# Graph attention on one core: the values of group 1 in other banks, the first group transposed in three steps, a warm-up before the first weights

## What is computed

```python
h = jnp.maximum(_layernorm(x, axis=-1), 0.0)
output = jnp.einsum('bni,io->bno', feature, weight)
q = jnp.einsum('bni,io->bno', feature, wq)
k = jnp.einsum('bni,io->bno', feature, wk)
alpha = jnp.einsum('bno,bmo->bnm', q, k)
alpha = jnp.maximum(alpha, 0.0) * (graph != 0).astype(alpha.dtype)
alpha = jax.nn.softmax(alpha, axis=1)
return jnp.einsum('bnm,bmo->bno', alpha, output)   # feature is h; x is added
```

## Time and profile before

| | before |
|---|---|
| median of 3 runs | 421.62 us (420.26 to 421.87) |
| profiled execution | 420.8 us, of which the span of the trace is 419.0 us |
| PE busy | 406.6 us (97%) |
| DVE busy | 282.9 us (68%) |
| ACT busy | 253.3 us (60%) |
| POOL busy | 298.2 us (71%) |
| chain that ended last | PE 81%, POOL 9%, DMA 3%, DVE 3% |
| DMA in the first slice (10.5 us) | 286 GB/s |

### The profile page before, as it was taken

How to read it: one execution, slowest core, us unless ns; L and a number is a source line. 1 busy time by engine, 2 the same in 40 slices (tenths; PEclk the granted TensorE clock), 3 DMA queues, 4 the chain that set the end, 5 groups by cost and what they waited for, 6 DMA issues and landing times.

```text
span 419.0 us, 9187 instructions
## 1 busy us (share of the span) xinstructions
PE 406.6 (97%) x3499; PEld 314.8 (75%) x3499; DVE 282.9 (68%) x504; ACT 253.3 (60%) x517; POOL 298.2 (71%) x315
## 2 busy tenths in 40 slices
PE   5999997999999999999999999999999999999996
PEld 4434543779889797979889797979889797978452
DVE  4786566475866768685876768676777677456353
ACT  4478774657485666667485666667586765523421
POOL 0379887979979797979879797979889796130320
PEclk9999999999999999999999999999999999999999
DMA  7965748996969797896978598996988599261022
GB/s 286 364 91 97 194 81 212 202 219 177 191 216 178 221 165 206 199 210 178 196 238 157 154 213 219 194 207 180 187 251 151 157 228 221 51 107 59 0 103 100
DMA packets 157368, 73.97 MB, mean 177 GB/s; under 512 B 131216, under 2 KB 139408, under 8 KB 157328
## 3 DMA queue, kind: packets, MB, share of 16 engines
q1 hardware_dynamic: 156752, 72.37, 75.5%
q10 hardware_dynamic: 576, 1.05, 0.7%
HBM read 24.12 MB, written 16.78 MB: 98 GB/s over the span
## 4 chain that ended last, share of the span: by engine, by line
PE 81%; POOL 9%; DMA 3%; DVE 3%; ACT 1%; SPq 1%; issue 1%; DVEq 0%; POOLq 0%; ACTq 0%
PE bank L1041 9%; PE bank L1027 9%; PE bank L1026 9%; PE bank L1042 9%; PE bank L1024 9%; PE bank L1039 9%; PE s_bank L1055 3%; PE s_bank L1053 3%; PE s_bank L1054 3%; POOL hn_lo L375 2%; PE bank L1060 2%; PE bank L1062 2%; PE bank L1061 2%; DMA x_sb<-in_x 2%; POOL hn_lo L401 2%; PE bank L1160 2%
## 5 line engine op out<-in xcount | busy, mean ns | idle before, releaser
L375 POOL TENSOR_TENSOR hn_lo<-h,hn_hi 128x512 f16<-128x512 f32 x64 | 73.4, 1159 | 41.0 <-ACT hn_hi L512 40.7
L502 ACT ACTIVATE h<-x_sb,shift,rstd 128x512 f32<-128x512 f32 x64 | 49.8, 803 | 51.4 <-POOL shift L370 51.4
L401 POOL TENSOR_TENSOR hn_lo<-s,hn_hi 128x512 f16<-128x512 f32 x52 | 58.6, 1159 | 0.0
L1024 PE MATMUL bank<-hT_hi,mt_hi 128*128 128x256 f16 x208 | 56.7, 273 | 0.0
L1027 PE MATMUL bank<-hT_hi,mt_lo 128*128 128x256 f16 x208 | 56.7, 273 | 0.0
L1041 PE MATMUL bank<-wt_lo,hT_hi 128*128 128x256 f16 x208 | 56.7, 273 | 0.0
L1042 PE MATMUL bank<-wt_hi,hT_lo 128*128 128x256 f16 x208 | 56.7, 273 | 0.0
L1026 PE MATMUL bank<-hT_lo,mt_hi 128*128 128x256 f16 x208 | 56.7, 273 | 0.0
L1039 PE MATMUL bank<-wt_hi,hT_hi 128*128 128x256 f16 x208 | 56.7, 273 | 0.0
L517 ACT ACTIVATE hn_hi<-s 128x512 f16<-128x512 f32 x52 | 32.5, 628 | 36.4 <-POOL s L390 23.9
L407 POOL TENSOR_TENSOR probs<-exps,row_inv 128x512 f32<-128x512 f32 x16 | 16.8, 1049 | 47.3 <-DVE row_inv L829 47.3
(11 more groups left out here) (142 smaller groups left out, 1153.4 us busy)
## 6 DMA issues: line engine op xcount, KB each, us to landing
x_sb<-in_x SPq DMA_DIRECT2D x16, 1024.0 KB, 5.5
out_h<-x_sb SPq DMA_DIRECT2D x64, 256.0 KB, 2.1
adj_sb<-in_adj SPq DMA_DIRECT2D x16, 256.0 KB, 5.4
w_sb<-in_L_gnn_weight SPq DMA_DIRECT2D x1, 1024.0 KB, 11.4
hn_lo<-in_L_gnn_wk ACTq DMA_DIRECT2D x2, 256.0 KB, 3.9
hn_lo<-in_L_gnn_wk SPq DMA_DIRECT2D x2, 256.0 KB, 3.7
hn_hi<-in_L_gnn_wq SPq DMA_DIRECT2D x2, 256.0 KB, 6.3
hn_hi<-in_L_gnn_wq ACTq DMA_DIRECT2D x2, 256.0 KB, 6.9
```

Of the source, the lines that this page charges most:

```text
L375: nc.gpsimd.tensor_tensor(hn_lo[:, s, b], h[:, b], hn_hi[:, s, b], ALU.subtract).then_inc(h_split, 1)
L401: nc.gpsimd.tensor_tensor(low, s32[:, f], high, ALU.subtract).then_inc(s_split, 1)
L502: nc.scalar.activation(h[:, b], x_sb[:, s, b], ACT.Relu, bias=shift[:, b:b + 1], scale=rstd[:, b:b + 1]).then_inc(h_made, 1)
L1024: nc.tensor.matmul(o, bh[:, k, cols], ah[:, :, k], start=first and c == 0 and k == 0, stop=False, skip_group_check=True)
```

## The change

Five edits:

1. Fourteen transposes of the identity by itself are issued on PE before the first weights, into the bank that w_top is transposed into later. Nothing reads them.
2. Row block 0 of wk and of wq comes in two halves of 64 rows, one from SP's queue and one from ACT's; their semaphore is waited for at 32.
3. The blocks of group 0 are transposed by six DMAs in place of eight: block 0, block 1, and blocks 2 and 3 together, each high and low. The high one waits only for hn_hi.
4. v of group 1 goes to banks 0 to 3, each block waiting for tT_lo of its own bank; the wait for out_read of all four blocks moves behind them, ahead of the scores of group 1. Period 2 waits for v_lo of blocks 0 to 2 in place of all four.
5. On ACT the high part of t of group 1, bank 3, is made ahead of those of sums S2 and S4 of group 2.

```diff
+    WARM = 14
-        V_BANK = [bank[VB][:], bank[VE][:], bank[FREE][:], bank[TA][:]]
+        def v_bank(g):
+            return M_BANK if g == 1 else [bank[VB][:], bank[VE][:], bank[FREE][:], bank[TA][:]]
...
-            def transpose_first(b):
-                sp.wait_ge(h_split, b + 1)
-                sp.dma_start_transpose(hT_hi[:, 0, b], hn_hi[:, 0, b]).then_inc(hT0_landed[b], 16)
-                sp.dma_start_transpose(hT_lo[:, 0, b], hn_lo[:, 0, b]).then_inc(hT0_landed[b], 16)
+            def transpose_first(b, n, landed):
+                sp.wait_ge(h_hi_made, b + n)
+                sp.dma_start_transpose(hT_hi[:, 0, b:b + n].rearrange("p b k n -> p (b k) n"),
+                                       hn_hi[:, 0, b:b + n].rearrange("p b d -> p (b d)")).then_inc(landed, 16)
+                sp.wait_ge(h_split, b + n)
+                sp.dma_start_transpose(hT_lo[:, 0, b:b + n].rearrange("p b k n -> p (b k) n"),
+                                       hn_lo[:, 0, b:b + n].rearrange("p b d -> p (b d)")).then_inc(landed, 16)
...
-            for r in (0, 2):
-                sp.dma_start(wk_sb[:, r], wk[r * N:(r + 1) * N, :]).then_inc(wk_loaded[r], 16)
-            for r in (0, 2):
-                sp.dma_start(wq_sb[:, r], wq[r * N:(r + 1) * N, :]).then_inc(wq_loaded[r], 16)
+            sp.dma_start(wk_sb[0:N // 2, 0], wk[0:N // 2, :]).then_inc(wk_loaded[0], 16)
+            sp.dma_start(wk_sb[:, 2], wk[2 * N:3 * N, :]).then_inc(wk_loaded[2], 16)
+            sp.dma_start(wq_sb[0:N // 2, 0], wq[0:N // 2, :]).then_inc(wq_loaded[0], 16)
+            sp.dma_start(wq_sb[:, 2], wq[2 * N:3 * N, :]).then_inc(wq_loaded[2], 16)
...
+            act.dma_start(wk_sb[N // 2:N, 0], wk[N // 2:N, :]).then_inc(wk_loaded[0], 16)
             for r in (1, 3):
                 act.dma_start(wk_sb[:, r], wk[r * N:(r + 1) * N, :]).then_inc(wk_loaded[r], 16)
+            act.dma_start(wq_sb[N // 2:N, 0], wq[N // 2:N, :]).then_inc(wq_loaded[0], 16)
...
             hi_of_whole_t(1, 2)
+            hi_of_whole_t(1, 3)
             hi_of_sum(2, 0, 2, S2)
             hi_of_sum(2, 0, 3, S4)
-            hi_of_whole_t(1, 3)
...
             pe.wait_ge(ident_made, 1)
+            for k in range(WARM):
+                nc.tensor.transpose(top_bank[:, N * (k % K):N * (k % K + 1)], ident[:], ident[:])
...
-            pe.wait_ge(t_split, K + 1)
-            for b in range(GB):
-                pe.wait_ge(out_read, b + 1)
-                whole_product_v(1, b)
+            for b in range(GB):
+                pe.wait_ge(t_split, K + b + 1)
+                whole_product_v(1, b)
+            pe.wait_ge(out_read, GB)
             scores(1, 1, quadrants=False)
-            pe.wait_ge(v_split, 2 * GB)
+            pe.wait_ge(v_split, GB + TE + 1)
```

More of the change, by code:

```diff
@@ L232, in graph_attention_kernel @@
         s_split = sem("s_split")
-        hT0_landed = [sem(f"hT0_landed{b}") for b in range(GB)]
+        hT0_landed = [sem(f"hT0_landed{b}") for b in range(3)]
         hT_landed = [sem(f"hT_landed{s}") for s in range(2)]
@@ L329, in _ @@
             load_x(2)
-            for b in range(GB):
-                transpose_first(b)
+            transpose_first(0, 1, hT0_landed[0])
+            transpose_first(1, 1, hT0_landed[1])
+            transpose_first(2, 2, hT0_landed[2])
             transpose_h(1)
@@ L601, in hi_of_whole_v @@
                     act.wait_ge(out_filled, GB * g)
-                nc.scalar.activation(v_hi[:, b], V_BANK[b], ACT.Copy, scale=T_SCALE).then_inc(v_hi_made, 1)
+                nc.scalar.activation(v_hi[:, b], v_bank(g)[b], ACT.Copy, scale=T_SCALE).then_inc(v_hi_made, 1)
             def hi_of_whole_t(g, c):
@@ L709, in _ @@
             hi_of_h(2, 0, 2)
-            act.wait_ge(hT0_landed[3], 2 * 16)
             hi_of_h(2, 0, 3)
@@ L873, in lo_of_whole_v @@
                 vec.wait_ge(v_hi_made, GB * g + b + 1)
-                nc.vector.scalar_tensor_tensor(v_lo[:, b], V_BANK[b], T_SCALE, v_hi[:, b], ALU.mult,
+                nc.vector.scalar_tensor_tensor(v_lo[:, b], v_bank(g)[b], T_SCALE, v_hi[:, b], ALU.mult,
                                                ALU.subtract).then_inc(v_split, 1)
@@ L890, in _ @@
             for r in range(K):
-                vec.wait_ge(wk_loaded[r], 16)
+                vec.wait_ge(wk_loaded[r], 32 if r == 0 else 16)
                 weight_max(wk_sb[:, r], w_max[:, 2, r:r + 1])
             for r in range(K):
-                vec.wait_ge(wq_loaded[r], 16)
+                vec.wait_ge(wq_loaded[r], 32 if r == 0 else 16)
                 weight_max(wq_sb[:, r], w_max[:, 1, r:r + 1])
@@ L1116, in transpose_wk @@
             def transpose_wk(r):
-                pe.wait_ge(wk_loaded[r], 16)
+                pe.wait_ge(wk_loaded[r], 32 if r == 0 else 16)
                 if r >= 2:
@@ L1124, in transpose_wq @@
             def transpose_wq(r):
-                pe.wait_ge(wq_loaded[r], 16)
+                pe.wait_ge(wq_loaded[r], 32 if r == 0 else 16)
                 if r < 2:
@@ L1143, in whole_product_v @@
             def whole_product_v(g, b):
-                s, dst = g % 2, V_BANK[b]
+                s, dst = g % 2, v_bank(g)[b]
                 for k in range(K):
@@ L1184, in _ @@
                 whole_product_v(0, b)
-            pe.wait_ge(hT0_landed[GB - 1], 2 * 16)
             pe.wait_ge(m_split, K)
```

## The result

| | before | after |
|---|---|---|
| median, first measurement | 421.53 us | 424.32 us (423.07 to 425.52, 6 runs), ratio 1.0071 [1.0057, 1.0085] |
| measured once more | 421.09 us | 423.83 us (423.33 to 425.37, 6 runs), ratio 1.0078 [1.0061, 1.0096] |
| profiled execution, span | 420.8, 419.0 us | 424.12, 422.3 us |

A forecast was written before the change was run, and what follows sets the result against it. POOL's chain up to p_lo, not PE's gaps, was taken to decide the change; PE bounds the rest. Terms -0.25, -0.93, +1.35 and +0.45 us gave +0.6, 421.4 us, named as 421.7 on the median's scale; range 419.6 to 423.7.

The forecast's parts named there:

- Two half transfers of 0.125 MB each move from SyncE's queue to ACT's: At the weight loads: ACT's last wq row 0.9 us later; with warm-up, PE 0.1 gained, bounds 0.5 lost to 0.13 gained.
- Rival D: At the front: halves and warm-up delay M, group 0's scores no earlier; +0.85 to +1.35, about 422.8 us; chance 0.09.
- What bounds the kernel, and that PE's gaps don't count: From 54.57 to 89.75 us POOL's chain decides; PE's gains there are spent waiting at outs(1) unless p_lo comes earlier.
- Rival B: At PE's idle times: the closed gaps reach the end, 3.5 us faster, 418.1 us; chance 0.06.
- Three steps for group 0, and what reaches POOL (0.25): Group 0's transposes: 0.86 us PE wait goes, PE 0.7 to 1.15 us earlier; POOL's normalise(0) gains 0.25, bounds 0 to 1.15.
- Values in t's banks: Group 1: PE's 2.67 us wait goes, mt_lo starts 3 to 4 us earlier; POOL's chain -0.93, +1.35, +0.45.
- the lows: POOL's four lows of sums: three mt_lo collide there, 0.45 us each, 1.35 us added to POOL's chain.
- the small operations: POOL's layernorm operations: 0.93 us saved, no longer disturbed; the fourth mt_lo meets one, 0.45 us added.
- rival C: After outs(1): longer PE waits make PE fall to 1.2 GHz; 4.3 us slower, 425.9 us; chance 0.08.
- The rule on transposes: At the front: by the rule the fourteen transposes are pure delay, 0.6 us; the prediction said the trace disagrees.
- The sum: POOL's chain, 54.57 to 89.75 us: -0.25, -0.93, +1.35, +0.45, together +0.6 us; p_lo at 90.3 instead of 89.7.
- The signs: Right: shift(3) ending at 70.2 to 71, mt_lo starting near 63; for rival D, a wait at L1174's successor ending after 17.7.

The follow-up runs named there:

- e15: The kernel before with only wk's row 0 in halves of 64 rows on both queues; 423.22 us, ratio 1.0048.
- e19: The kernel before with wk's row 0 in halves, issued second on each queue; 422.91 us, ratio 1.0049.
- e5: The kernel before with row 0 of wk and of wq in halves of 64 rows, both on SP's queue; 423.60 us, ratio 1.0061.
- e2: The kernel before with only the half transfers of wk and wq on both queues; 422.56 us, ratio 1.0038.
- e11: The kernel before with row 0 of wk and wq halved by columns (128 rows of 1 KB) on both queues; 421.85 us, ratio 1.0020.
- e16: The kernel before with only wq's row 0 in halves on both queues; 421.36 us, ratio 1.0008.
- e13: The kernel before with the 14 transposes of the identity alone; 421.48 us, ratio 1.0010.
- e3: The kernel before with only group 1's v in the other banks and the ACT order that goes with it; 421.58 us, ratio 1.0005.
- e4: As e3, but the four mt_lo moved to where POOL waits for ACT; 419.94 us, ratio 0.9966.
- e14: The kernel before with six transposes of group 0 instead of eight, alone; 421.59 us, ratio 1.0011.
- e18: e4 with six transposes of group 0; 419.99 us, ratio 0.9973.
- e1: The kernel after with row block 0 of wk and wq in one transfer again; 421.92 us, ratio 1.0011.
- e17: The kernel after with mt_lo late as in e4; 421.71 us, ratio 1.0020.

## Why the prediction was wrong

**The failed step is "Two half transfers of 0.125 MB each move from SyncE's queue to ACT's".** The prediction took only their bytes for a cost: wq's last row 0.9 us later, nothing beyond, 0.1 us gained by the warm-up and at most 0.5 lost. It held the rate (286 GB/s) and x's landing fixed. The runs showed two things in its place. The maximum of wq's last row came 2.78 us later and not 0.9, past the start of the statistics; the prediction named this way of losing, and had its size wrong. And x itself landed later: in the earlier trace rows DVE already waited 1.41 us for x, so nothing hides that. In e15, e19 and e5 the statistics wait 0.8 to 1.4 us for x behind the last maximum, in e2 they follow the maximum directly.

Over the profiles, w_top came at 16.79 to 17.69 us in ten with wk in whole rows (mean 17.14) and at 18.12 to 19.07 in seven where both queues begin with a half of wk (mean 18.39): 1.25 us lost. e19, with the halves second, has 18.24, the column halves of e11 17.59. By e2, e5, e15, e16 and e19 the loss goes with halves of 64 rows in the opening. The halves alone cost 1.6 us [1.0, 2.2] (0.38%), wk's alone 2.0 [1.5, 2.6]. The 0.1 us of the warm-up isn't seen either (e13).

Rival D ("the change doesn't do what it says at the front") was this case, by the halves and not by the warm-up. It had 0.09 and a price of 0.85 to 1.35 on the whole, and even D took the loads of x as on time.

The other steps:

- *What bounds the kernel, and that PE's gaps don't count*: right. e3 and e4 both close the residual's gap, and only e4 is faster. Rival B is refuted.
- *Three steps for group 0, and what reaches POOL (0.25)*: near. The weight load's wait for hT_lo fell from 1.35 to 0.48 us, and from w_top to row_inv it took 36.64 to 36.68 us in all profiles with six transposes, 36.86 to 37.26 in those with eight. A benefit on the time isn't shown by any run: alone they measured +0.11% (e14), added to e4 nothing (e18).
- *Values in t's banks*: the mechanism right, with mt_lo in the lows; the prices too. Predicted -0.93 + 1.35 + 0.45 = +0.87 on the stretch, measured +0.92 (e3) and +1.04 (after). By terms: the lows +1.34 for +1.35, the small operations -0.30 (69.86 to 72.50 is 2.64 us) for -0.93 + 0.45 = -0.48. The wait before period 2 was said to be 2 us and is 2.84; the one before outs(1) was said to be 2 to 3 us and is 1.03.
- *The clock*: PE waited 2.84 us, longer than any wait in the earlier trace rows, and L1034's matmul after it takes the 0.28 us that it took before; rival C didn't come.
- *The rule on transposes*: by the rule of the Trainium skill, "TensorE: Matmul & The Clock Gate", Part 4, that transposes don't engage the full clock, the fourteen were a pure delay. After them wk's transposes took 272 ns where they took 421 before. PE had run nothing but transposes up to then, so the trace disagrees. The row that the prediction took for this, the 272 ns at 13.3 us, doesn't show it by itself, since from 9.8 on PE also ran products of M. The delay of 0.4 us (4.2 to 4.63) was hidden.
- *The sum*: -0.25 + 0.87 = +0.6 was forecast for p_lo. Measured: +1.79 (front) - 0.36 + 1.04 = +2.47. On the scale on which the rivals were priced (421.62 us) +0.6 gives 422.2, not the 421.7 that was named.
- *The signs*: the sign of D came: L1187, which waits for w_top, went at 19.30 us, and D asked for a time after 17.7. shift(3) ended at 72.50 and not by 71, and mt_lo started at 65.04 and not near 63; in e1, with the front on time, it started at 63.02.

Summed from the parts alone, halves 0.38%, transposes 0.11, warm-up 0.10 and banks 0.05 give 0.64% against 0.71 and 0.78 measured, within the intervals. But e1 has the last three together at 0.11%, not at 0.26. With the halves of e2 that makes 0.49%, which is 0.22 to 0.29 (0.9 to 1.2 us) short of the whole, about as much as the intervals allow. Whether the halves cost more in the changed kernel than alone stays open.

Open is why the DMA rate falls in the opening. Between 3.0 and 3.5 us it was 94 GB/s in the first profile after and 279 in the second, 389 before. Shown is that halves of wk's first row block in the opening do it, not by which mechanism. Open too is why the times with the banks lie below what the stretch makes of them (e3 +0.2 for +0.92, e4 -1.4 for -0.60). One part is that the profile of before caught a short stretch: nine profiles without the banks have 33.92 to 34.47 (mean 34.20), five with var_eps at 0.20 to 0.21 us and four with it at 0.74 to 0.76, as mt_lo misses that operation by a little or meets it. Against the mean e3 has +0.68 and e4 -0.84, and 0.5 to 0.6 us are left. e17 deviates the other way: 1.25 - 0.36 - 0.88 = 0.0 us for a measured +0.8 [0.3, 1.4]. No run was made for it.

## What to carry to other kernels

Where the first work waits for loads, price every edit of the load sequence by what it does to the last loads that are waited for, and not by when the edited transfer is needed. Before closing a gap of an engine, look which operations it pulls forward and what they will meet: here four operations with two inputs in SBUF lengthened POOL's stretch by 1 us beside its lows and shortened it by 0.6 in its idle time. Splitting the first load by columns measured +0.20% and by partitions +0.38%, with overlapping intervals; not splitting it removed the loss.

## What was not expected of the hardware

- Issuing a transfer of 64 partitions (2 KB each) took 0.48 to 0.58 us. A weight row block of 128 partitions with none of 64 ahead of it took 0.40 to 0.47, whether with 2 KB or with 1 KB in each. Two whole rows behind ACT's half of wk took 1.33 us to issue, without the half 0.90 (issues on ACT's queue, after and then before):

```profile
0.74 0.58 ACTq L498 DMA_DIRECT2D hn_lo<-in_L_gnn_wk  x1
1.35 1.33 ACTq L500 DMA_DIRECT2D hn_lo<-in_L_gnn_wk  x2
```
```profile
0.73 0.90 ACTq L490 DMA_DIRECT2D hn_lo<-in_L_gnn_wk  x2
```

- The first 12 us moved 300 to 309 GB/s in the ten profiles with wk in whole rows, and 266 to 278 in the seven where both queues begin with such a half. With the halves second (e19) it was 290.
- mt_lo beside POOL's lows: four take 5.2 to 5.4 us instead of 2.5, that is 0.7 us more each, while POOL's four lows lose 1.34 (0.90 in e3). DVE lost two to three times what these lows did.
